# New orders for the four compute engines in a deep local-attention stage, and V's moves issued in two parts

## The reference

```python
def attn_layer(x, Wqkv, qs, ksc, Wo):
    q, k, v = split_heads(x @ Wqkv)          # 16 heads of 64
    q, k = l2norm(q) * qs, l2norm(k) * ksc
    q = q * cos * scale + rotate_half(q) * sin * scale
    k = k * cos / scale + rotate_half(k) * sin / scale
    return local_attention(q, k, v) @ Wo     # windows of 32, each with the one before
for i in range(6):
    x = attn_layer(shift_tokens(x), Wqkv[i], ...) + x
    x = ffn_layer(shift_tokens(x), ...) + x  # layer norm, 128 -> 2*341, gelu gate, -> 128
```

## Time and profile before

| | |
|---|---|
| three runs, us | 4786.8, 4783.35, 4789.63 (median 4786.8) |
| profiled execution, its own time / span, us | 4788.12 / 4786.4 |
| granted TensorE clock, mean | 0.961 |
| busy over the span, us | PE 4232.6 (88%), DVE 4071.3 (85%), ACT 3053.7 (64%), POOL 3012.7 (63%) |
| first and last feed-forward block's statistics, us | 1508.7, 4756.5 |

### The profile page before, as it was taken

How to read it: one execution, slowest core, us unless ns; L and a number is a source line. 1 busy time by engine, 2 the same in 40 slices (tenths; PEclk the granted TensorE clock), 3 DMA queues, 4 the chain that set the end, 5 groups by cost and what they waited for, 6 DMA issues and landing times.

```text
span 4786.4 us, 164817 instructions
## 1 busy us (share of the span) xinstructions
PE 4232.6 (88%) x70208; PEld 3350.3 (70%) x70208; DVE 4071.3 (85%) x6282; ACT 3053.7 (64%) x5515; POOL 3012.7 (63%) x1586
## 2 busy tenths in 40 slices
PE   5698699999668999999999998999989999999996
PEld 4566377877656777777777777777767777777775
DVE  4344699999788999999989999899998999989995
ACT  3365333333156777777777777777777777777773
POOL 0222566666267767677776777767776677766772
PEclk9699799999889999999999999999999999999998
DMA  1234000000023234232332323333242332433322
GB/s 50 78 127 141 0 1 0 0 0 0 19 54 76 58 70 95 63 81 62 75 88 64 84 58 90 80 67 75 60 101 66 67 77 58 96 74 67 75 58 74
DMA packets 237661, 302.78 MB, mean 63 GB/s; under 512 B 92500, under 2 KB 127832, under 8 KB 236504
## 3 DMA queue, kind: packets, MB, share of 16 engines
q1 hardware_dynamic: 221752, 247.08, 22.7%
q0 software_dynamic: 15264, 46.14, 3.1%
HBM read 50.37 MB, written 28.84 MB: 17 GB/s over the span
## 4 chain that ended last, share of the span: by engine, by line
DVE 41%; PE 14%; issue 9%; POOL 5%; ACT 4%; SPq 1%; DMA 0%; POOLq 0%; DVEq 0%; ACTq 0%
DVE raw L1906 10%; DVE raw L1913 8%; DVE mx L1964 3%; DVE E L1970 3%; DVE ss L1900 3%; PE shared L1565 2%; PE acc L1672 2%; DVE den L1977 2%; PE sco L1640 2%; POOL spare L2129 2%; POOL raw L2137 2%; DVE hT L2027 2%; PE shared L1567 2%; PE shared L1566 1%; ACT raw L1783 1%
## 5 line engine op out<-in xcount | busy, mean ns | idle before, releaser
L2137 POOL TENSOR_TENSOR raw<-raw,rs 128x1024 f32<-128x1024 f32 x384 | 794.4, 2069 | 887.4 <-DVE rs L1934 551.8
L2129 POOL TENSOR_TENSOR spare<-raw,table 128x1024 f32<-128x1024 f32 x384 | 969.7, 2536 | 79.1 <-DVE raw L1913 63.3
L1906 DVE TENSOR_TENSOR raw<-raw,table 128x1024 f32<-128x1024 f32 x384 | 667.9, 1739 | 87.1 <-POOL spare L2129 85.5
L1913 DVE TENSOR_TENSOR raw<-raw,spare 128x1024 f32<-128x1024 f32 x384 | 725.5, 1889 | 13.2
L1783 ACT ACTIVATE raw<-shared 128x512 f32<-128x512 f32 x768 | 463.2, 603 | 311.2 <-PE shared L1567 280.2
L1565 PE MATMUL shared<-wqkv_lo,xT_hi 128*128 128x512 f32 x1152 | 550.0, 477 | 57.1 <-DVE xT_lo L1943 49.0
L2154 POOL TENSOR_TENSOR E<-E,rden 128x512 f32<-128x512 f32 x384 | 544.2, 1438 | 30.8 <-DVE rden L1979 30.8
L1900 DVE TENSOR_REDUCE ss<-spare 128x16 f32<-128x1024 f32 x384 | 463.8, 1208 | 62.3 <-ACT spare L1788 61.9
L1620 PE MATMUL trn<-ident,raw 128*128 128x128 f32 x3072 | 485.2, 281 | 6.9 <-POOL raw L2137 3.4
L1567 PE MATMUL shared<-wqkv_hi,xT_hi 128*128 128x512 f32 x1152 | 462.6, 402 | 0.0
L1566 PE MATMUL shared<-wqkv_hi,xT_lo 128*128 128x512 f32 x1152 | 462.2, 401 | 0.0
(11 more groups left out here) (208 smaller groups left out, 9678.4 us busy)
## 6 DMA issues: line engine op xcount, KB each, us to landing
Vw<-V SPq DMA_DIRECT2D x1344, 128.0 KB
xs<-X SPq DMA_DIRECT2D x144, 128.0 KB, 2.6
Vw<-V SPq DMA_DIRECT2D x192, 64.0 KB
e_plain<-in_L_ffn_W SPq DMA_DIRECT2D x16, 704.0 KB, 4.6
split_hi<-e_high POOLq DMA_DIRECT2D x16, 704.0 KB, 5.9
split_lo<-e_low POOLq DMA_DIRECT2D x16, 704.0 KB, 7.0
wqkv_hi<-split_hi POOLq DMA_DIRECT2D x30, 256.0 KB, 3.1
wqkv_lo<-split_lo POOLq DMA_DIRECT2D x30, 256.0 KB, 3.2
```

The lines of the kernel that those rows point to most:

```text
L1906: dve.tensor_tensor(x, x, table[:, part, 0, k][:, None, :].to_broadcast([P, H, HD]), ALU.mult).then_inc(cos_part, 1)
L1913: dve.tensor_tensor(x, x, t2[:, part], ALU.add).then_inc(summed, 1)
L2129: pool.tensor_tensor(dst, src, by[:, None].to_broadcast([P, H, 2, 32]), ALU.mult).then_inc(sin_part, 1)
L2137: pool.tensor_tensor(x, x, rs[:, at:at + H][:, :, None].to_broadcast([P, H, HD]), ALU.mult).then_inc(rotated, 1)
```

## The change

Every table of steps of the deep stage is set anew (only TURNED_FOR, STEPS, LAST_PARTS, SCORE_STEPS and OUT_STEPS stay), and with them the order of the instructions of PE, ACT, DVE and POOL, among them the steps at which weight chunks are loaded. No compute instruction is added or removed. In move_v the one wait for four drains becomes two: the first eight DMAs, which read the first 512 columns of V, wait for two drains, the last eight for four.

```diff
--- before.py
+++ after.py
@@ -1158,40 +1158,40 @@
 BLOCKS = DEPTH * GROUP
 PROJ_ORDER = [(k, part, a) for k in range(2) for part in range(2) for a in range(2)] \
     + [(0, 2, 0), (1, 2, 0), (0, 2, 1), (1, 2, 1)]
-PROJ_STEPS = (-15, -14, -13, -12, -11, -10, -9, -8, -5, 7, 11, 12, 15)
+PROJ_STEPS = (-15, -14, -13, -12, -11, -10, -9, -8, -7, 8, 13, 14, 15)
 TURN_ORDER = [(0, 0, 0), (0, 1, 0), (1, 0, 0), (1, 1, 0), (0, 0, 1), (0, 1, 1), (1, 0, 1), (1, 1, 1)]
-TURN_STEPS = (4, 6, 7, 8, 9, 13, 14, 15)
+TURN_STEPS = (3, 6, 7, 8, 9, 12, 14, 15)
 TURNED_FOR = (4, 8)
 STEPS = 16
 LAST_PARTS = ((0, 3), (3, 6), (6, 7), (7, 8))
-SINE_STEPS = (-10, -9, -4, 3)
-REDUCE_STEPS = (-9, -8, -7, -3)
-COSINE_STEPS = (-5, -4, 2, 7)
-NEWTON_STEP = -2
-SCALE_STEPS = (-2, 1, 3, 5)
+SINE_STEPS = (-8, -3, -2, -1)
+REDUCE_STEPS = (-12, -9, -4, -3)
+COSINE_STEPS = (-7, -6, -1, 5)
+NEWTON_STEP = 0
+SCALE_STEPS = (0, 1, 2, 10)
 SCORE_STEPS = (0, 5)
-HIGHEST_STEPS = (4, 10)
-EXP_STEPS = (5, 12)
-TOTAL_STEPS = (9, 15)
-NORM_STEPS = (8, 16)
-FLIP_STEPS = (11, 18)
-MIX_STEPS = (13, 21)
-DRAIN_STEPS = (15, 22)
+HIGHEST_STEPS = (4, 9)
+EXP_STEPS = (5, 9)
+TOTAL_STEPS = (7, 12)
+NORM_STEPS = (14, 16)
+FLIP_STEPS = (9, 17)
+MIX_STEPS = (11, 22)
+DRAIN_STEPS = (18, 23)
 OUT_STEPS = (25, 26)
-ADD_ATTN_STEP = 28
-B_STAT_STEP = 0
+ADD_ATTN_STEP = 29
+B_STAT_STEP = 2
 B_POWER_STEP = 1
-B_AWAY_STEP = 7
+B_AWAY_STEP = 6
 B_NORMAL_STEP = 8
-B_TURN_STEP = 13
-B_AFFINE_STEP = 13
-B_LOW_STEP = 14
+B_TURN_STEP = 10
+B_AFFINE_STEP = 10
+B_LOW_STEP = 15
 B_HIDDEN_STEPS = (17, 20, 24)
 B_GELU_STEPS = (17, 20, 24)
-B_GATED_STEPS = (17, 23, 27)
-B_OUT_STEP = 28
-B_ADD_STEP = 31
-CHUNK_STEPS = (22, 23, 24, 29, 45, 47)
+B_GATED_STEPS = (19, 21, 25)
+B_OUT_STEP = 25
+B_ADD_STEP = 30
+CHUNK_STEPS = (27, 30, 31, 31, 49, 49)
 ROWS = 16
 
 
@@ -1458,8 +1458,8 @@
 
             def move_v(n, par):
 
-                sp.wait_ge(v_drained, count(VS * n + VS))
                 for hp in range(2):
+                    sp.wait_ge(v_drained, count(VS * n + 2 * hp + 2))
                     v = V[:, :, hp * 512:hp * 512 + 512]
                     own, back = 64 * hp + WIN, 64 * hp
                     for g in range(4):
```

## The result

The changed kernel took 4818.97 us in the median of four executions (4816.38 to 4820.74), the kernel before 4788.22 beside it (4783.35 to 4794.13): 1.0065 times as long, interval 1.0052 to 1.0078, some 31 us slower. The forecast was 4762.

The account below looks back on a forecast made before the run. The port, on which DVE's and POOL's large operations take turns, was taken to bound the kernel. From 4788.1 us, 19 for full pairs and 6 for weight chunks came off: 4763, as a median 4762, range 4715 to 4825.

Parts of the forecast that it names:

- PE and ACT: PE's reordered work and its wait for the low part of x: costed at 0, bounds 0 and +1.5 us a pair.
- the port: What DVE's and POOL's large operations take turns on, one at a time; a serial loop of 34.41 us in steps 0 to 15.
- first half: Half of a pair with steps 0 to 15: charted at 35.0 us against 34.41 before, +0.6.
- second half: Other half of a pair, without statistics, power or L2019: 33.85 us against 35.08 or 34.63, -1.0 in the mean.
- The chart: Timeline of DVE and POOL operations in the new order from Newton's start: 68.85 us a pair against 69.27, -0.42.
- a weight chunk: Two issues on POOL's queue: one chunk less on the loop, 1.2 us at each of five layer changes, -6 us.
- The reduction: DVE's last square reduction before Newton leaves the loop, beside POOL's sine 1k and norm 1: -1.2 us in each half.
- The power instruction: On POOL between scalings 0k and 1q: loses its cover and costs 1.01 us, with 2.0 as the other end.
- Rival B: Slower: POOL's power instruction costs 2.0 us in place, pair 69.85, 4808 us; chance 0.10.
- Rival D: Faster: POOL's power instruction holds the port and was paid all along, pair 67.8, 4715 us; chance 0.08.
- Rival A: PE's wait for x's low part delays scores and DVE's maximum; 3.4 us late in one half gives 4825; chance 0.20.
- Rival C: No change: norm 0 and cosine 0q always fall the bad way, +0.4 us a pair, 4782 us; chance 0.15.

Follow-up runs that it names:

- e1: Changed kernel plus five unread 128x512 bf16 products on PE, first half of each pair, before the scores that wait for DVE's subtraction, with a bank-free wait: 4769.51 us.
- e5: As e1, with two extra products instead of five: 4774.95 us, 0.9972 of the kernel before.
- e7: e1 with the power instruction moved behind the scaling of 1q on POOL (B_POWER_STEP 1 to 3): 4765.26 us, 0.9956 of the kernel before.
- e13: The changed kernel itself, run once more beside e14: 4813.35 us, 1.0042 of the kernel before.
- e14: The changed kernel with V's moves again behind a single wait for all four drains: 4807.25 us, 1.0042 of the kernel before.
- e12: Changed kernel with DVE's statistics at step 4, the power instruction behind scaling 1q, and e1's five products: 4831.1 us, 1.0087 of the kernel before.
- e6: Changed kernel plus five extra products once a pair, ahead of mix 0, where PE does not wait for DVE's subtraction: 4799.99 us, 1.0025 of the kernel before.
- e10: Changed kernel with PE's turn of next x and DVE's Newton one step earlier, plus e1's five products: 4845.91 us, 1.0124 of the kernel before.

## Why the prediction was wrong

**The failed step is "PE and ACT".** It counted that PE needs 63.5 of 68.85 us, found room for 5.4 us of waits and wrote "Costed at 0 because the port hides it". The wait itself is as large as the step foresaw: 0.85 and 1.62 us in the first half, well within the room. Two things were missing. No term stood for the granted clock, which the tables of before gave as 0.99 and which was taken as given. And the path no longer went through the port but through PE for more than half of a pair (e1's chain), so what PE lost was not hidden: with 7 us at the lower level in a pair, the last products and scores are late and DVE waits 3.34 us instead of 0.65. Against e1 the cost is 31 us in the 25 pairs away from a change of layer and 19 in the 20 at one, 50 in all. The step's own upper bound, +1.5 in each of 45 pairs or 68 us, would have held it; it was the value taken, 0, that was wrong. That the lower clock costs this is shown for the 31 us, by slow and fast pairs of one trace; that PE's new waits are what lets it fall is supported by e1 and e5 and not isolated.

**The sum without it.** The forecast was -25 us on the profiled execution. e1's profiled execution took 4763.62 us of its own time against 4788.12, -24.5, but it is the fastest of its five; by medians it is 4769.51 against 4789.19, -19.7. That the sum comes so near is partly luck: the regular pairs gave less than forecast, the changes of layer twice as much as all else, and some of it is clock, not order. By its steps:

| step | forecast | shown by e1, clock mostly full |
|---|---|---|
| first half, from scaling 0q to scaling 0q, us | 35.0 | 35.08 |
| second half | 33.85 | 34.09 |
| regular pair | 68.85 | 69.17 to 69.25 |
| gain in a regular pair against 69.27 | 0.42 | 0.02 to 0.10 |
| spacing from the power instruction to scale 1q | 1.0 | 0.97 |
| gain over the 25 pairs away from a change of layer | 10.5 | 5.5 |
| gain over the four pairs at a change of layer | 2.9 | 2.4 in the mean of five, 0.2 to 5.4 |

The halves come from POOL's order of time, e1; the first is the pair of 69.17 less the second, 3393.65 less 3359.56:

```profile
3359.56 5.64 POOL L2142 TENSOR_TENSOR raw<-raw,rs 128x1024 f32<-128x1024 f32 x3 [5.95 <-DVE rs L1939]
...
3393.65 3.77 POOL L2142 TENSOR_TENSOR raw<-raw,rs 128x1024 f32<-128x1024 f32 x2 [5.42 <-DVE rs L1939]
3397.52 1.01 POOL L2189 TENSOR_TENSOR small<-small,halves 128x4 f32<-128x4 f32 x1
3398.49 1.90 POOL L2142 TENSOR_TENSOR raw<-raw,rs 128x1024 f32<-128x1024 f32 x1
```

The chart was right to 0.3 us in a pair, but the gain to be found was only 0.4, so three quarters of it went in that rest. The forecasts of the last two lines are 0.42 in every pair and 1.2 more at a change of layer. The first change compares 73.19, 70.74, 70.32 and 70.21 us before with 70.77, 71.46, 70.40 and 70.22 in e1. At the fifth, where the gain is 5.4, two of the four pairs before have a clock below 0.97. So no run shows the 1.2 us of a weight chunk by itself.

**The bound.** That the kernel before turned on the port was argued from the chain and the durations and isn't contradicted: POOL leaves the chain with the change, and its instructions are held up less. But the new order does not turn on it: e1's chain has no piece of POOL, and e7 moves the power instruction for nothing. The chart compared only DVE with POOL, and let DVE's maximum find its scores ready.

**The reduction and V's moves.** The reduction left the stretch before scaling 0q as forecast. The moves are worth nothing, as forecast (e13 and e14). ACT's drain of V now waits 26.2 us instead of 0.9, always for PE. In e1, where PE is less late, it is 34.9, so it goes with the new order and not with the clock.

**The power instruction.** 1.01 was the right choice in this order. Rival B's 2.0 is real in another one (1.91 in e12), when the instruction meets a DVE product that has begun before it. Rival D is not shown: the instruction is now off the path. The Trainium skill, SBUF — State Buffer, "SBUF: two separate sides", says that GpSimd and a DVE instruction with two SBUF inputs exclude each other. The trace agrees in one direction only: in e12 the power instruction, begun behind DVE's product, ends 0.86 us after it, but DVE's sum begins at 3369.41 beside the power instruction and is not held, as in the earlier trace rows with the earlier trace rows.

**Rival A** named the right place, PE behind the low part of x and then the scores, and had +38 us, a chance of 0.20 and nearly the right time. Its reason was another: it wanted the low part 2 us late in a half. Here waits of 0.85 and 1.62 us went with it by way of the clock, so that its time was nearly right is in part luck. The signs named the right rows as well, with too high a mark: DVE's wait for scores is 68.1 us over some 47 halves, 1.4 each, and PE's for the low part 30.2, less than 1, where "more than 2 us a half" was asked. Rival C, the pieces cancel, is near the truth for the regular pairs alone.

**A sign wrongly derived.** POOL's wait for Newton was to shrink below 4.5 us a time. It is 263.6 over 47, 5.6. The chart itself has POOL free at 32.05 and scaling 0q at 35.0 + 3.1, a wait of 6.05, and e1 shows 5.95.

## What to carry to other kernels

Where PE is busy 9 tenths of a stage, a new wait of one or two microseconds on it can have a second price, a lower clock for the microseconds after it; ask of each new order which waits of PE it makes, and leave the bounds open upward for what PE's slower products delay. In such a place a few products that nobody reads, put in the wait, are a quick test: if the kernel gets faster with more work, the clock is the first suspect. Then compare pairs of high and low clock in one trace, which is the cleaner proof, and put the same products in the kernel before as well. And chart every engine of the loop before a sum of 0.4 us in 69 is trusted, since here the path ran over PE for more than half of a pair, and PE was left out.

## What the runs showed of the hardware

**The clock.** It fell soon behind waits of PE of 0.85 and 1.62 us in one pair and stayed behind 0.85 and 1.96 us in the next, in a stage where PE is busy 64 to 67 of 69 to 71 us. A fall lasted about 7 us at a granted clock of 0.51 and made the pair 2.05 us longer. Of 45 pairs 23 had a clock below 0.97 in the changed kernel and 24 in e13; 1 with five products in the wait (e1), 4 with two (e5), 19 with five elsewhere (e6). Executions of one program differ by up to 26 us (e14). The Trainium skill, TensorE: Matmul & The Clock Gate, "HAM oscillation — how this bites in real kernels", tells of waits between bursts of products after which the clock falls in each round. This trace shows the same kind of fall, but behind waits for another engine in the place of a DMA, which are much shorter than the work between them, and in about half of the pairs rather than in all.

**Small DVE instructions are held by large POOL ones.** The groups of instructions by line, 2615 to 4273 us, have this one of the kernel before,

```profile
L2012 DVE TENSOR_SCALAR small<-mv 128x4 f32<-128x4 f32 x24 | 16.3, 679 | 0.8
```

and this one of the changed kernel:

```profile
L2012 DVE TENSOR_SCALAR small<-mv 128x4 f32<-128x4 f32 x23 | 26.6, 1157 | 0.8
```

The same instruction takes 0.17 us in e12 at 3368.08. In the changed kernel it stands beside scaling 0k, ends with it (3362.01, and POOL's scaling at 3361.99), and delays the maximum behind it: half a microsecond more in a pair than before (1157 against 679 ns), on the very path that makes PE wait. It has one tensor input and a length of 4, so it takes neither size nor a second input for a DVE instruction to be held.

**Left open:** why the clock falls in one pair and not in the next with the same waits; whether e1 works by the filled wait, by more work on PE or by its added wait for the drains; what the same products would give in the kernel before; and what holds e10's scores.
